# Centring and scaling in one GpSimd instruction, a projection moved forward on TensorE, and bias sums moved to an earlier pass

## The reference

```python
xn = (x - mean(x)) / sqrt(var(x) + 1e-5)                 # per token
Q, K = elu(xn @ Wq.T + bq) + 1, elu(xn @ Wk.T + bk) + 1  # 16 heads of 16
V = xn @ Wv.T + bv
KV, K_sum = einsum('bshd,bshe->bhde', K, V), K.sum(axis=1)
Z = 1 / (einsum('bshd,bhd->bsh', Q, K_sum) + 1e-6)
attn = einsum('bshd,bhde,bsh->bshe', Q, KV, Z) @ Wo.T + bo
probs = softmax(xn @ gate_w)                # 8 experts
g, m = top_k(probs over tokens, 256)        # each expert takes 256 tokens of each sequence
ffn = scatter_add(g * (gelu(xn[m] @ w1) @ w2)).astype(bfloat16)
out = x + attn + ffn
```

## Time and profile before

| | us |
|---|---|
| median of 3 runs | 1908.34 |
| lowest, highest | 1907.77, 1910.2 |
| the profiled execution: its time | 1909.48 |
| the profiled execution: its span | 1907.7 |
| mean granted TensorE clock | 0.997 of full speed |
| DMA, mean over the span | 177 GB/s |

### The profile page before, as it was taken

One profiled execution on the slowest core, in us unless ns is written; L12 is line 12 of the kernel. 1 busy time (PEld: TensorE's weight loads), 2 busy tenths in 40 slices (PEclk: granted clock), 3 DMA queues, 4 the chain that ended last, 5 costly groups with the idle time before them and its releaser, 6 DMA issues. The chain is left out here.

```text
span 1907.7 us, 39892 instructions
## 1 busy us (share of the span) xinstructions
PE 1837.9 (96%) x13916; PEld 1281.4 (67%) x13916; DVE 1348.1 (71%) x2585; ACT 1256.1 (66%) x2014; POOL 1064.7 (56%) x973
## 2 busy tenths in 40 slices
PE   5899999999999999999999999999999999999998
PEld 3677777777766666666666666666666666666666
DVE  6678989898857777655888876655666556555657
ACT  5788888676546666666656666566666666666664
POOL 5545454645335555555665566765665655555563
PEclk9999999999999999999999999999999999999999
DMA  6698889899665555567666667576766657676757
GB/s 166 183 238 251 234 249 282 231 254 239 191 172 122 122 140 117 146 169 174 156 152 153 166 143 177 118 184 156 188 153 161 172 135 183 155 186 156 182 118 219
DMA packets 449188, 338.27 MB, mean 177 GB/s; under 512 B 225043, under 2 KB 430614, under 8 KB 449046
## 3 DMA queue, kind: packets, MB, share of 16 engines
q1 hardware_dynamic: 383958, 253.84, 48.0%
q0 software_dynamic: 48864, 66.88, 19.4%
q10 hardware_dynamic: 16224, 15.73, 2.5%
HBM read 185.61 MB, written 100.40 MB: 150 GB/s over the span
## 5 line engine op out<-in xcount | busy, mean ns | idle before, releaser
L2015 PE MATMUL pY<-w2s,hid 128*128 128x256 f16 x6144 | 758.2, 273 | 14.2 <-DVE yo L1875 10.5
L2000 PE MATMUL pH<-xgT,w1s 128*128 128x512 f16 (+1 forms) x3120 | 747.6, 376 | 1.3 <-PEq L330 1.3
L2015 PEld LDWEIGHTS pY<-w2s,hid 128*128 128x128 f16 x6144 | 598.1, 98 | 199.6 <-DVE yo L1875 15.9
L1859 DVE SCALAR_TENSOR_TENSOR hid<-gel,cur,hid 128x512 f16<-128x512 f32 (+1 forms) x520 | 441.7, 850 | 400.9 <-ACT hid L1798 303.0
L1795 ACT ACTIVATE gel<-pH,cur 128x512 f32<-128x512 f32 (+1 forms) x520 | 353.9, 680 | 498.9 <-PE pH L2000 415.2
L1768 POOL DMA_INDIRECT acc<-yo,idx x254 | 410.8, 1618 | 446.2 <-DVE yo L1875 371.0
L2000 PEld LDWEIGHTS pH<-xgT,w1s 128*128 128x128 f16 x3120 | 305.2, 98 | 252.4 <-DMA xgT<-xg 1.6
L1798 ACT ACTIVATE hid<-gel,cur 128x512 f16<-128x512 f32 (+1 forms) x520 | 372.0, 715 | 17.1
L225 POOL DMA_INDIRECT xg<-table,idx x256 | 280.1, 1094 | 111.9 <-issue 59.3
L745 POOL TENSOR_TENSOR phk<-phik,phk 128x256 f16<-128x256 f32 x128 | 92.0, 719 | 196.0 <-ACT phk L827 195.9
L1875 DVE TENSOR_SCALAR yo<-pY,gains,cur 128x256 f32<-128x256 f32 x256 | 121.6, 537 | 13.5 <-PE pY L2015 12.3
(11 more groups left out here) (249 smaller groups left out, 1992.0 us busy)
## 6 DMA issues: line engine op xcount, KB each, us to landing
stage<-in_w SPq DMA_DIRECT2D x160, 512.0 KB, 5.6
xring<-in_x SPq DMA_DIRECT2D x16, 1024.0 KB, 6.7
x2ring<-in_x SPq DMA_DIRECT2D x16, 1024.0 KB, 7.2
table<-xhl SPq DMA_DIRECT2D x32, 512.0 KB, 5.0
mix<-x2ring SPq DMA_DIRECT2D x32, 512.0 KB
acc<-zeros SPq DMA_DIRECT2D x16, 1024.0 KB, 5.1
fmix<-mix SPq DMA_DIRECT2D x48, 256.0 KB
facc<-acc SPq DMA_DIRECT2D x48, 256.0 KB
```

The costliest lines, as they stand in the source:

```text
L1859: v.scalar_tensor_tensor(out=hid[:, hc % 4, 1, w], in0=gel[:, hc % 2, w], scalar=cur[expert_of(b, q)][:, 1:2], in1=hid[:, hc % 4, 0, w], o ...
L2000: last = t.matmul(pH[hc % 4][:, tok], w[:, aw, c, hc * P:(hc + 1) * P], xgT[i][:, ad, c, tok], start=k == 0 and c == 0, stop=k == 2 and c ...
L2015: last = t.matmul(pY[s // 2][:, s % 2, :], hid[:, hc % 4, ad, s * P:(s + 1) * P], w[:, aw, hc, :], start=hc == 0 and k == 0 and s % 2 == 0 ...
```

## The change

Three edits.

1. **Centring and scaling.** `norm` makes (variance + 1e-5) * 2048^-2, so that rpow is already 2048 / standard deviation. `centre` subtracts the mean and multiplies by rpow in one instruction with two pointer scalars, and for tile 0 waits for rpow. `rstd` and DVE's `root_of` are gone, 16 instructions. `high` is a plain copy to float16 with no scale operand, and `low` a tensor_tensor subtraction in place of scalar_tensor_tensor.
2. **Order on PE.** P6 stands directly behind P5, ahead of S3, and S4 moves from behind Q2 to behind Q3.
3. **Bias sums of the last group.** They move from bodies 4 and 7 to body 3: 16 instructions over 2 tiles each, one behind each scatter-add, in place of 8 over 4 tiles. The semaphore of the lmix loads is split in two.

```diff
@@ norm, root, centre (POOL)
-                    g.tensor_scalar(veps[:, :], moments[:, :, 1], 1e-5, None, ALU.add).then_inc(veps_done, 1)
+                    g.tensor_scalar(veps[:, :], moments[:, :, 1], 1e-5, XSCALE ** -2, ALU.add, ALU.mult).then_inc(veps_done, 1)
...
-                    pool.wait_ge(rstd_done, at(rstd_done, n, -1))
...
                     if j == 0:
-                        pool.wait_ge(aggr_done, at(aggr_done, n))
+                        pool.wait_ge(rpow_done, at(rpow_done, n))
                     if n > 0 or j >= HALF:
                         pool.wait_ge(lo_done, at(lo_done, n, j - HALF))
-                    g.tensor_scalar(xm[:, j % HALF, :], xring[:, n % XR, j, :], moments[:, j, 0:1], None, ALU.subtract).then_inc(xm_done, 1)
+                    g.tensor_scalar(xm[:, j % HALF, :], xring[:, n % XR, j, :], moments[:, j, 0:1], rpow[:, j:j + 1],
+                                    ALU.subtract, ALU.mult).then_inc(xm_done, 1)
@@ high (ACT)
-                    a.activation(xhl[h][:, jj, 0, :, :].rearrange("p c t -> p (c t)"), xm[:, j % HALF, :], ACT.Copy,
-                                            scale=rstd[:, j:j + 1]).then_inc(hi_done, 1)
+                    a.activation(xhl[h][:, jj, 0, :, :].rearrange("p c t -> p (c t)"), xm[:, j % HALF, :], ACT.Copy).then_inc(hi_done, 1)
@@ root_of, low (DVE)
-                def root_of(n):
-                    if not (isinstance(n, int) and n == 0):
-                        dve.wait_ge(lo_done, at(lo_done, n, -1))
-                    dve.wait_ge(rpow_done, at(rpow_done, n))
-                    v.tensor_scalar(rstd[:, :], rpow[:, :], XSCALE, None, ALU.mult).then_inc(rstd_done, 1)
...
-                    v.scalar_tensor_tensor(
-                        out=xhl[h][:, jj, 1, :, :].rearrange("p c t -> p (c t)"), in0=xm[:, j % HALF, :],
-                        scalar=rstd[:, j:j + 1], in1=xhl[h][:, jj, 0, :, :].rearrange("p c t -> p (c t)"),
-                        op0=ALU.mult, op1=ALU.subtract).then_inc(lo_done, 1)
+                    v.tensor_tensor(xhl[h][:, jj, 1, :, :].rearrange("p c t -> p (c t)"), xm[:, j % HALF, :],
+                                    xhl[h][:, jj, 0, :, :].rearrange("p c t -> p (c t)"), ALU.subtract).then_inc(lo_done, 1)
@@ body of the first stage (PE)
                     for j in range(NT):
-                        project(n, j)
+                        if j != 6:
+                            project(n, j)
+                        if j == 5:
+                            project(n, 6)
...
                         if j in (6, 7):
                             q_part(n, j - 4)
+                        if j == 7:
+                            sum_kv(n, 4)
                         if j >= 2:
-                            sum_kv(n, j - 2)
+                            if j != 6:
+                                sum_kv(n, j - 2)
@@ body of the second stage (POOL)
                         for s in tiles_of(b, q):
                             g.indirect_dma_start(
                                 acc, bass.IndirectOffsetOnAxis(ap=idx[q][:, s:s + 1], axis=0), yo[i][:, s, :], None,
                                 compute_op=ALU.add).then_inc(added_end if in_halves(b, q) else added[i], 16)
-                        if isinstance(b, int) and b in (G1, G2 - 1):
-                            if b == G1 and q == 0:
-                                pool.wait_ge(lmix_in, at(lmix_in, 0, LP - 1))
-                            tiles = lmix[:, piece_of(q if b == G1 else q + LP // 2), :]
-                            g.tensor_tensor(tiles, tiles, bo_all[:, :].unsqueeze(1).to_broadcast([P, HALF, D]), ALU.add).then_inc(lbo_done, 1)
+                            if isinstance(b, int) and b == G1 - 1:
+                                pool.wait_ge(lmix_in[q % 2], at(lmix_in[q % 2], 0, 2 * (q // 2) + 1))
+                                tiles = lmix[:, 2 * HALF * q + 2 * s:2 * HALF * q + 2 * s + 2, :]
+                                g.tensor_tensor(tiles, tiles, bo_all[:, :].unsqueeze(1).to_broadcast([P, 2, D]), ALU.add).then_inc(lbo_done, 1)
```

More of the change, by code:

```diff
@@ L342, in block_program @@
             rpow = sb("rpow", [P, NT], F32)
-            rstd = sb("rstd", [P, NT], F32)
             minus_half = sb("minus_half", [P, NT], F32)
@@ L464, in block_program @@
             rpow_done = event("rpow_done")
-            rstd_done = event("rstd_done", credit=1)
             xm_done = event("xm_done", per=NT, credit=1)
@@ L693, in _ @@
                 g.memset(ones[:, :], 1.0).then_inc(consts, 1)
-                for ev in (*row_out, *mix_out, *piece_done, xm_done, veps_done, rstd_done, *x_turned, k_done, klo_done, kv_used,
+                for ev in (*row_out, *mix_out, *piece_done, xm_done, veps_done, *x_turned, k_done, klo_done, kv_used,
                            kv_out, logits_done, q_proj, qraw_done, q_done, shifted, den, kv_turned, qz_done, mix_done,
@@ L859, in _ @@
                 act.wait_ge(consts, at(consts, 0, 4))
-                act.wait_ge(rstd_done, at(rstd_done, 0))
                 for j in range(HALF):
@@ L882, in _ @@
                         if nxt and j == HALF:
-                            act.wait_ge(rstd_done, at(rstd_done, n, 1))
                             high(n + 1, 0)
@@ L1010, in bias_blocks @@
                     last.then_inc(bvo_step, 1)
-                def root_of(n):
-                    if not (isinstance(n, int) and n == 0):
-                        dve.wait_ge(lo_done, at(lo_done, n, -1))
-                    dve.wait_ge(rpow_done, at(rpow_done, n))
-                    v.tensor_scalar(rstd[:, :], rpow[:, :], XSCALE, None, ALU.mult).then_inc(rstd_done, 1)
                 def low(n, j):
                     h, jj = divmod(j, HALF)
-                    if j == 0:
-                        dve.wait_ge(rstd_done, at(rstd_done, n))
                     dve.wait_ge(hi_done, at(hi_done, n, j))
-                    v.scalar_tensor_tensor(
-                        out=xhl[h][:, jj, 1, :, :].rearrange("p c t -> p (c t)"), in0=xm[:, j % HALF, :],
-                        scalar=rstd[:, j:j + 1], in1=xhl[h][:, jj, 0, :, :].rearrange("p c t -> p (c t)"),
-                        op0=ALU.mult, op1=ALU.subtract).then_inc(lo_done, 1)
+                    v.tensor_tensor(xhl[h][:, jj, 1, :, :].rearrange("p c t -> p (c t)"), xm[:, j % HALF, :],
+                                    xhl[h][:, jj, 0, :, :].rearrange("p c t -> p (c t)"), ALU.subtract).then_inc(lo_done, 1)
                 def gate_logits(n, h):
@@ L1163, in _ @@
                 weight_maxima()
-                root_of(0)
                 fold_maxima()
@@ L1216, in body @@
                             gate_logits(n, 0)
-                            if nxt:
-                                root_of(n + 1)
                         if j == 7:
@@ L1537, in block_program @@
             fin_bo = event("fin_bo")
-            lbo_done = event("lbo_done", per=LP)
+            lbo_done = event("lbo_done", per=2 * LP)
             fin_done = event("fin_done")
-            lmix_in = event("lmix_in", per=LP, step=16)
+            lmix_in = [event(f"lmix_in{i}", per=4, step=16) for i in range(2)]
             added_end = event("added_end", step=32)
@@ L1715, in body @@
                             for i in (2 * q, 2 * q + 1):
-                                sp.dma_start(lmix[:, piece_of(i), :], last_rows[0][:, piece_of(i), :]).then_inc(lmix_in, 16)
+                                sp.dma_start(lmix[:, piece_of(i), :], last_rows[0][:, piece_of(i), :]).then_inc(lmix_in[q % 2], 16)
                 for h in range(2):
@@ L1892, in finish_last @@
                     if i == 0:
-                        dve.wait_ge(lbo_done, at(lbo_done, 0, LP - 1))
+                        dve.wait_ge(lbo_done, at(lbo_done, 0, 2 * LP - 1))
                     if i % 2 == 0:
```

## The result

| | before | after |
|---|---|---|
| median, us | 1907.49 (20 runs) | 1910.9 (20 runs) |
| lowest, highest | 1906.06, 1910.2 | 1907.54, 1916.8 |
| the profiled execution: time, span | 1909.48, 1907.7 | 1908.87, 1907.1 |
| mean granted clock | 0.997 | 0.994 |
| first stage, to the first pH matmul | 535.9 | 544.0 |

The ratio is 1.0016, with an interval of 1.001 to 1.0022: a tenth or two of a per cent slower, which is what the text above calls no change. The forecast was 1901.5, and 1910.9 lies outside its range of 1890 to 1908.5. The large change moved the time little because two effects cancel: the second stage is 8.6 us shorter, the first 8.1 us longer.

A forecast was written before the change was run, and what follows sets the result against it. PE, 96% busy, was taken as the bound, so only its idle time and waits count. Terms -10.4 + 7.5 - 2.2 - 1.8 = -6.9 us took the profiled execution from 1909.5 to 1902.6, the median from 1908.3 to 1901.5; range 1890 to 1908.5.

The forecast's parts named there:

- Bias sums gone from bodies 4 and 7: Second stage, POOL's list: without the sums ahead of gathers and finishing sum, body 4 gains 5.2 us and body 7 8.1.
- Body 3: Second stage: the 16 added sums fit into POOL's wait for yo with 1.6 us to spare; 0.3 us for holding DVE.
- Rival E: The sums in body 3 do not fit and POOL's lateness reaches the gathers: at most 2 us; chance 0.17 with C.
- One thing is late next: Start of body 4: finishing loads wait for body 3's later last scatter-add, costing 2.6 us once, between 0 and 3.1.
- Tile 6: First stage: P6, moved ahead of S3, waits for tile 6's transpose DMA in eight bodies: 7.5 us lost, between 0 and 10.0.
- O0's wait: First stage, PE: the 0.23 us wait before O0 goes in 10 bodies, a gain of 2.2 us.
- `rstd` and `low`: First stage, DVE: dropping rstd shortens none of PE's longest waits; low, 0.04 us shorter each, gains 1.8 us, between 0 and 2.4.
- Centring: First stage, POOL: the centring with two pointer scalars takes 1.1 us and, with P6 ahead of S3, costs nothing.
- C: Everything late: all 10.0 us at tile 6 and body 3's sums holding DVE, 1906 us; chance 0.17 with Rival E.
- D: First stage, POOL: the two-scalar centring is long, deciding from 1.26 us on; at 1.6 us 1921, slower; chance 0.08.
- A: First stage: tile 6's transpose lands in time for P6, so the 7.5 us loss falls away: 1894.0 us; chance 0.20.

The follow-up runs named there:

- edit 2 alone: The kernel before with only PE's new order (P6 ahead of S3, S4 behind Q3): 1916.7 us, 1.0048 against before.
- edit 1 alone: The kernel before with only the centring and scaling edit: 1906.77 us, 1.0001 against before.
- the later load: The changed kernel with the 1 MB x2ring load on SP's queue moved behind the transposes of tiles 6 and 7 and the second store of rows: 1895.81 us.
- constant scalar: The changed kernel with the centring's second scalar the constant XSCALE instead of the pointer rpow: 1913.55 us in its one run.
- the last version: All three edits, x2ring load behind tiles 6 and 7, four bias sums moved from body 3's last quarter into bodies 4 and 7: 1889.97 us, 0.9906 against before.

## Why the prediction was wrong

- **Bias sums gone from bodies 4 and 7 (-5.2, -8.1).** Right: -4.8 and -8.1.
- **Body 3 (+0.3).** Right in effect: DVE was held, by up to 2.4 us at a time, and it cost nothing. POOL's waiting held the sums with 1.05 us to spare and not 1.6, since each added 1.49 us and not 1.26 (10.20 us from first to last scatter-add for 5.73, three sums). Rival E's sign, body 3 slower than 85 us, did appear (87.9 for 84.6), but the excess is all in its last quarter, the next item.
- **"One thing is late next" (+2.6).** Right place, wrong road, undersized: 3.6. The step had the loads late behind the last scatter-add, which three sums delay by 3.8 us. That scatter-add did come 4.5 us later in its quarter (10.2 us behind the first for 5.7), but what held the finishing sum was POOL's own list, with the fourth sum ahead of the gathers, which the step left out. The cast stood 3.70 us, more than the upper end of 3.1.
- **Tile 6 (+7.5, between 0 and 10.0).** This is the step that failed. The subtraction body by body gave 10.0, and P6's waits are 10.7 in the changed kernel and 11.0 with edit 2 alone. That the sums agree so well is partly luck, since single bodies are off by up to 1.6 us. I then took off a quarter because "a stall of 2.7 us gives the crowded DMA queue time to catch up before bodies 3 and 4". It did not in sum: body 2 did wait less than priced, but body 3, priced at 1.5, waited 2.62 (1.57 with edit 2 alone). The upper end of the term was not an end either, for it held the waits alone. The clock adds 2.8 us in body 9. The kernels in which P6 waited 0.7 us or less in that body kept the clock there.
- **O0's wait (-2.2).** Right in kind, too small: where the tile is there, edit 2 gains 5.0 us, 0.46 a body. The 0.23 read off the brackets was 0.40 from start to start. That DVE was what O0 waited for is not shown: the row says "issue".
- **`rstd` and `low` (-1.8).** Within its bounds of 0 to -2.4: edit 1 alone measured -0.3 (-1.5 to +1.9 by its interval); body 6 got 0.44 us shorter but body 2 0.7 and body 9 0.6 longer.
- **Centring (1.1 us, at nothing).** It took 1.23, and the argument for 1.1, "only the second pointer is new", was wrong: three quarters of the cost are the second operation. That P6 hides it was right. Without this cover S3 waited 0.33 us, where I had said 0.2.
- **The rivals.** C, everything late, was the one that came nearest: it gave 1906 and had P6's 10.0 in full. It still lacked the clock. D had its point of decision at 1.26 us, and 1.23 stayed just under it; ACT's waits for `xm` did grow, from 18.8 to 48.7 us, and edit 1 alone shows that they cost nothing that can be measured. A, tile 6 in time, is the state that the later load brings about: 1894.0 forecast, 1895.81 measured, and this too is partly luck, for edit 2's gain was taken 2.8 us too small and those of edits 1 and 3 some 3 us too large.

In sum: the second stage was forecast at -10.4 and gave -8.6. The first was forecast at +3.5 (7.5 - 2.2 - 1.8) and gave +8.1. With the 1.8 us of the second stage that is 6.4 us of error. Of the first stage's 4.6, P6's waits are 3.2 (10.7 for 7.5), the clock 2.8 and edit 1 1.5; against them stand 2.8 of edit 2's larger gain. The parts as measured, 10.7 + 2.8 - 5.0 - 0.3 = 8.2, fit the 8.1, though some come from traces and some from medians. The other 3 us between 1901.5 and 1910.9 are the executions that were profiled: I put the median 1.1 us under the profiled execution of before, while the changed kernel's profiled execution was 2.0 us under its own median. Why its runs spread so much was not settled.

## What to carry to other kernels

Moving a step forward on the busiest engine moves forward its demand for data, so look at what the queue that brings them has in front of them, and move that too: here one bulk load with time to spare made the difference between 9.6 us lost and 5.0 gained. When each body's lateness can be read off the trace, take the sum as it stands, without a discount for things catching up, and add a price for the clock where PE would stand for some microseconds: here it was 2.8 us, once. A wait in front of matmuls is read from start to start, not from the brackets. POOL's sums held up DVE alone as well as in a row, so they belong where nothing critical stands behind DVE's instruction, and not in the last quarter ahead of the finishing sums.

## What the runs showed of the hardware

- The granted clock of PE fell to its lower level in body 9 after waits of 1.40 and 2.15 us (changed kernel), of 3.29 us (edit 2 alone), and of 0.84 and 2.69 us (constant scalar), and in no kernel where PE's waits for `xT` in that body came to 1.84 us or less. That is no rule for other places: it fell behind a single wait of 1.89 us in body 14 of the last version and in the second stage of edit 2 alone, and stayed at 2.4 GHz behind one of 1.90 at the same place of before and behind 2.62 in body 3 of the changed kernel. It was lower in body 1 of the changed kernel as well (0.81 from 70 to 75, behind a wait of 2.67 us for ACT), with the load later too (0.76).
- The changed kernel's runs spread over 9.3 us, those of before over 4.1, and the five with the load later over 2.0. The clock alone does not explain it: a mean granted clock of 0.989 stands beside the run of 1908.39 us and beside that of 1916.8.
- On GpSimd a second operation in the same tensor_scalar over 128 x 256 float32 takes 0.23 us more than one (medians 1.16 and 0.93), and a second pointer scalar 0.07 more (1.23).
- A DVE instruction of 0.75 us with two SBUF inputs took 3.56 beside three GpSimd sums issued back to back, 2.85 beside a single one of 1.83 us and 4.07 beside one of 2.94. Each time it ended 0.55 to 0.56 us behind the last sum.
- A GpSimd sum over 128 x 512 float32 takes 1.26 to 1.28 us, and 1.8 to 1.86 right behind a scatter-add; there it lengthened POOL's list by 1.49.
- `low` as a tensor_tensor has a least of 380 ns for 441 as scalar_tensor_tensor, and a median of 420 for 479; the gain of 60 is more than the 17 estimated in the prediction. Its most is still 910.
